# A four-block transformer kernel on one core: transposing the routing weights later, spreading a router's work over six expert steps, and the order of two multiplications

## What is computed

```
x = x + tanh(g_xattn[0]) * L0_xattn(layernorm(x), ctx)      # one attention over the context
x = x + tanh(g_ffn[0])   * L0_ffn(layernorm(x))             # ternary weights, inner width 704
x = x + tanh(g_xattn[1]) * L1_xattn(layernorm(x), ctx)      # 16 heads of 128, q and k rms-normed
x = x + tanh(g_ffn[1])   * L1_ffn(layernorm(x))             # 64 experts of width 64, 8 per token

# L1_ffn, h = its input
logits = h @ gate_w.T;  top-8;  W = softmax over the 8 chosen, 0 for the other 56
inter[e] = silu(h @ gu_w[e].gate) * (h @ gu_w[e].up) * W[:, e]
out = sum_e inter[e] @ dp_w[e].T + sigmoid(h @ sh_gate1_w.T) * shared_expert(h)
```

## Time and profile before

| | us |
|---|---|
| median of three runs | 646.48 |
| the profiled execution | 646.42 |
| its span in the trace | 644.6 |
| PE busy | 621.3 (96%) |
| DVE busy | 491.1 (76%) |
| ACT busy | 432.8 (67%) |
| POOL busy | 227.1 (35%) |
| mean DMA rate over the span | 86 GB/s |

### The profile page before, as it was taken

The page is one execution under the profiler, slowest core; times in us unless marked ns, Lnnn a source line. Parts: engine busy times, 40 slices in busy tenths (PEclk is TensorE's granted clock), DMA queues, the critical chain, the costliest instruction groups (busy, mean ns, idle before and its releaser), DMA issues.

```text
span 644.6 us, 11859 instructions
## 1 busy us (share of the span) xinstructions
PE 621.3 (96%) x3697; PEld 531.6 (82%) x3697; DVE 491.1 (76%) x1141; ACT 432.8 (67%) x1103; POOL 227.1 (35%) x262
## 2 busy tenths in 40 slices
PE   7888898999999999999989999999999999999997
PEld 5766687999999999999988887877887788888886
DVE  4999998767777778778886687877777677777775
ACT  5896998888888888888889434555444454444442
POOL 5576775766666666656654001000000000000000
PEclk9999999999999999999999999999999999999999
DMA  8420130110000000000003254436555245554440
GB/s 278 144 74 26 53 121 25 36 40 2 2 2 2 2 1 2 1 2 1 2 9 116 83 162 137 149 99 195 165 162 160 83 131 190 162 161 146 155 124 34
DMA packets 24806, 55.42 MB, mean 86 GB/s; under 512 B 4081, under 2 KB 4785, under 8 KB 24625
## 3 DMA queue, kind: packets, MB, share of 16 engines
q1 hardware_dynamic: 24752, 54.78, 27.6%
HBM read 53.45 MB, written 1.31 MB: 85 GB/s over the span
## 4 chain that ended last, share of the span: by engine, by line
PE 68%; DVE 15%; ACT 8%; issue 5%; POOL 2%; DMA 1%; SPq 0%; DVEq 0%; ACTq 0%
PE bank L285 19%; PE bank L287 19%; PE bank L286 19%; PE bank L775 3%; PE bank L750 2%; ACT front_hi L1521 2%; ACT att L1288 2%; PE bank L742 2%; DVE inter L1888 2%; DVE prod L1861 1%; DVE front_lo L2094 1%; DMA x<-in_x_tok 1%; DVE w L1650 1%; DVE stats L1603 1%; DVE amax L1707 1%
## 5 line engine op out<-in xcount | busy, mean ns | idle before, releaser
L1327 ACT ACTIVATE inter_hi<-inter 128x512 fp32r<-128x512 f32 x63 | 39.9, 634 | 142.7 <-DVE inter L1888 142.7
L285 PE MATMUL bank<-xnT_hi,front_hi 128*128 128x512 f32 (+1 forms) x260 | 102.3, 393 | 0.0
L287 PE MATMUL bank<-xnT_hi,front_lo 128*128 128x512 f32 (+1 forms) x260 | 101.7, 391 | 0.0
L286 PE MATMUL bank<-xnT_lo,front_hi 128*128 128x512 f32 (+1 forms) x260 | 101.6, 391 | 0.0
L1892 DVE TENSOR_TENSOR inter_lo<-inter,inter_hi 128x512 fp32r<-128x512 f32 x63 | 43.6, 693 | 45.8 <-ACT inter_hi L1327 45.8
L1288 ACT ACTIVATE att<-bank,shift,rq 128x256 f32<-128x256 f32 x128 | 71.3, 570 | 0.6 <-DVE shift L1781 0.6
L498 POOL TENSOR_TENSOR rk<-msq,minus_half 128x4 f32<-128x4 f32 x32 | 33.1, 1034 | 89.7 <-DVE msq L1763 89.6
L514 POOL TENSOR_TENSOR att<-att,rowinv 128x512 f32<-128x512 f32 x60 | 62.0, 1053 | 7.5 <-DVE rowinv L1791 7.5
L1774 DVE TENSOR_REDUCE rowmax<-bank 128x2 f32<-128x512 f32 x64 | 43.7, 686 | 27.0 <-PE bank L287 26.9
L1861 DVE TENSOR_TENSOR prod<-gate_s,bank 128x512 f32<-128x512 f32 x63 | 43.2, 686 | 19.7 <-PE bank L287 17.3
L287 PEld LDWEIGHTS bank<-xnT_hi,front_lo 128*128 128x128 f32 x260 | 48.8, 188 | 11.3
(11 more groups left out here) (271 smaller groups left out, 1846.8 us busy)
## 6 DMA issues: line engine op xcount, KB each, us to landing
w_all<-w_rows SPq DMA_DIRECT2D x128, 128.0 KB, 2.9
raw<-in_expert_w SPq DMA_DIRECT2D x32, 384.0 KB, 3.6
wvo_raw<-in_expert_w SPq DMA_DIRECT2D x16, 384.0 KB, 3.6
e_more<-in_expert_w SPq DMA_DIRECT2D x16, 384.0 KB, 3.6
raw<-in_head_qk SPq DMA_DIRECT2D x8, 384.0 KB, 3.7
wvo_raw<-in_head_vo SPq DMA_DIRECT2D x8, 384.0 KB, 3.1
gate_raw<-in_gate_wT SPq DMA_DIRECT2D x1, 1408.0 KB, 10.1
x<-in_x_tok SPq DMA_DIRECT2D x2, 512.0 KB, 6.2
```

The lines of the kernel that those rows point to most:

```text
L285: pe.matmul(out, l_hi, r_hi_, start=start, stop=False, skip_group_check=True)
L286: pe.matmul(out, l_hi, r_lo_, start=False, stop=False, skip_group_check=True)
L287: return pe.matmul(out, l_lo, r_hi_, start=False, stop=stop, skip_group_check=True)
L1327: act.activation(inter_hi[:, slot, :], inter[:, slot, :], ACT.Copy).then_inc(a_Ihi, 1)
```

## The change

There are three edits, of order only: no instruction is added or removed, apart from where waits stand.

1. In group 28 the first half's weights are transposed behind `values(28)`, into bank 6 (QBK) and no longer bank 7. ScalarE copies them out at the end of its group 28, behind `o_hi`, and PE waits for both copies in group 29, in front of `turn_q(31)`, which writes bank 6.
2. The second half's router has one step more: best eight in step 12, subtraction and choice in step 13, the exponentials in ScalarE's step 14, the sum in step 15, the weights in step 16, transposed and copied behind step 17.
3. In the last pair silu is multiplied by the routing weight first and by up then, and both pieces are multiplied before the first low part is made.

```diff
@@ PE, group g
+                if g == 29:
+                    pe.wait_ge(a_wk, 2)
                 if g + 2 < GROUPS:
                     pe.wait_ge(a_sqQ, 4 * min(n, GROUPS))
                     turn_q(g + 2)
...
-                if g == 28:
-                    turn_weights(0, KBK)
...
-                if g == 28:
-                    pe.wait_ge(a_wk, 2)
                 if g + 2 < GROUPS:
                     turn_k(g + 2)
...
                 values(g)
+                if g == 28:
+                    pe.wait_ge(v_Qlo, 31)
+                    turn_weights(0, QBK)
@@ PE, step q
-                if q == 16:
+                if q == 17:
                     turn_weights(1, 3)
@@ ScalarE, group g
-                if g == 28:
-                    keep_rows(0, KBK)
-                    keep_shared(0, KBK)
...
                 if n < GROUPS:
                     raw_k(n)
+                if g == 28:
+                    keep_rows(0, QBK)
+                    keep_shared(0, QBK)
@@ ScalarE, step q
-                if q == 13:
-                    silu(1, q, q)
+                if q == 14:
+                    silu(0, q, q)
                     weight_exps(1)
                     act.activation(spare[:, :], tg[:, 0:1], ACT.Silu)
                     act.wait_ge(t_D, q - 1)
-                    high_inter(1, q)
+                    high_inter(0, q)
                     split_e(q + 2)
...
-                if q == 16:
+                if q == 17:
                     keep_rows(1, 3)
                     keep_shared(1, 3)
@@ VectorE, step q
                 if q == 11:
                     take_logits(1, 0, 2)
                     take_logits(1, 1, 3)
+                if q == 12:
                     best_eight(1)
+                if q == 13:
                     shift_logits()
-                if q == 12:
                     choose()
-                if q == 14:
+                if q == 15:
                     sum_weights(1)
-                if q == 15:
+                if q == 16:
                     weights()
@@ VectorE, last pair
+            def last_loaded(half, s):
+                cols = slice(half * 256, (half + 1) * 256)
+                dve.wait_ge(a_silu, s + 1)
+                dve.wait_ge(l_wall[3], EPAIRS // 2 * 32)
+                dve.tensor_tensor(prod[:, 1, cols], gate_s[:, 1, cols], w_all[:, 3, cols], ALU.mult).then_inc(v_mul1, 1)
+
             def last_up(half, bk, s):
                 cols = slice(half * 256, (half + 1) * 256)
-                dve.wait_ge(a_silu, s + 1)
+                dve.wait_ge(v_mul1, s + 1)
                 dve.wait_ge(t_U, 2 * EPAIRS + half)
-                dve.tensor_tensor(prod[:, 1, cols], gate_s[:, 1, cols], bank[bk][:, 0:256],
-                                  ALU.mult).then_inc(v_mul1, 1)
...
+                dve.tensor_tensor(inter[:, 1, cols], prod[:, 1, cols], bank[bk][:, 0:256], ALU.mult).then_inc(v_mul2, 1)
...
-            last_up(0, UB, 2 * EPAIRS + 1)
+            last_loaded(0, 2 * EPAIRS + 1)
+            last_up(0, UB, 2 * EPAIRS + 1)
+            last_loaded(1, 2 * EPAIRS + 2)
+            last_up(1, 3, 2 * EPAIRS + 2)
             last_low(0, 2 * EPAIRS + 1)
-            last_up(1, 3, 2 * EPAIRS + 2)
-            last_loaded(1, 2 * EPAIRS + 2)
             last_low(1, 2 * EPAIRS + 2)
```

More of the change, by code:

```diff
@@ L2154, in _ @@
                     last_steps(r, r % 2, q + 2, q, q // 4)
+            def last_loaded(half, s):
[3 more added lines that the diff above has]
+                dve.tensor_tensor(prod[:, 1, cols], gate_s[:, 1, cols], w_all[:, 3, cols], ALU.mult).then_inc(v_mul1, 1)
             def last_up(half, bk, s):
                 cols = slice(half * 256, (half + 1) * 256)
-                dve.wait_ge(a_silu, s + 1)
+                dve.wait_ge(v_mul1, s + 1)
                 dve.wait_ge(t_U, 2 * EPAIRS + half)
-                dve.tensor_tensor(prod[:, 1, cols], gate_s[:, 1, cols], bank[bk][:, 0:256],
-                                  ALU.mult).then_inc(v_mul1, 1)
[L2163 to L2166, removed]
                 dve.wait_ge(a_Ihi, 2 * EPAIRS)
-                dve.tensor_tensor(inter[:, 1, cols], prod[:, 1, cols], w_all[:, 3, cols], ALU.mult).then_inc(v_mul2, 1)
+                dve.tensor_tensor(inter[:, 1, cols], prod[:, 1, cols], bank[bk][:, 0:256], ALU.mult).then_inc(v_mul2, 1)
             def last_low(half, s):
@@ L2174, in last_low @@
                                   ALU.subtract).then_inc(v_Ilo, 1)
+            last_loaded(0, 2 * EPAIRS + 1)
             last_up(0, UB, 2 * EPAIRS + 1)
-            last_loaded(0, 2 * EPAIRS + 1)
+            last_loaded(1, 2 * EPAIRS + 2)
+            last_up(1, 3, 2 * EPAIRS + 2)
             last_low(0, 2 * EPAIRS + 1)
-            last_up(1, 3, 2 * EPAIRS + 2)
-            last_loaded(1, 2 * EPAIRS + 2)
             last_low(1, 2 * EPAIRS + 2)
```

## The result

| | us |
|---|---|
| before, median of 8 runs | 646.19 (645.59 to 647.63) |
| after, median of 8 runs | 648.75 (647.38 to 650.18) |
| ratio after / before, with its 95% interval | 1.0038 [1.0028, 1.0049] |
| the profiled execution after | 647.94 |
| its span in the trace | 646.2 |

The change makes the kernel slower by 0.38%, 2.56 us between the medians. 648.6 was forecast.

The account below looks back on a forecast made before the run. PE, busy 96% of the span, was taken as the bound. Terms +0.5 + 0.07 + 2.05 + 0.1 - 0.55 = +2.17 on 646.42 gave 648.6 us; range for 8 in 10: 646.0 to 649.8.

Parts of the forecast that it names:

- PE loses the wait before `turn_k(30)` and gets it back before `turn_q(31)`: Group 28: PE gains 1.75 us by `turn_k(30)`, then gives it all back waiting for ScalarE's second copy before `turn_q(31)`.
- The rival in which the wait really goes: Group 28: ScalarE's chain is shorter than 4.62 us, PE keeps the 1.12 us, time 647.0; chance 7%.
- Pair 3 is 1.4 us late at ScalarE, 0.5 us at PE: Edit 1: pair 3's load, issued 4.6 us later, stops ScalarE about 1.4 us; +0.5 for the edit in all.
- the -0.15 for a load in time: Edit 1, rival: pair 3's load lands in time, the edit gives -0.15 us, time 647.9; chance 15%.
- The bound of +0.7: Upper bound of edit 1's cost in us, around the taken +0.5; the lower bound was -0.15.
- VectorE's chain ends at 436.30, step 18 starts at 436.84: Edit 2: the second half's weights are ready 4.33 us later, yet PE starts step 18 only 0.07 us later.
- Without a hole: Second half's router before the change: VectorE has no hole from step 12 to the weights, 18.55 us.
- `w_keep` to DRAM at 439.7, the load at 442.3, landing at 445.5, `gate(20)` at 447.4, a hole of 2.05 us: Edit 2, SyncE's queue: the later copy delays pair 20's load; PE waits 2.05 us before `gate(20)`, bounds 0 and +3.3.
- The table change and the exponentials stay hidden: Edit 2, ScalarE: both start about 420.8, end at 424.1, before step 14's product at about 424.4; bounds 0 and +0.6.
- Pairs 21 to 23 at +0.1: Edit 2: these loads are issued as much later but had more time; range 0 to 0.3 us, taken 0.1.
- Last pair -0.55: Edit 3: PE's hole of 0.54 us before the last piece goes, -0.55 us, bounds -0.7 and 0.
- Sum +2.17: All edits together: +0.5 + 0.07 + 2.05 + 0.1 - 0.55 us against the profiled execution of 646.42, giving 648.6.

## Why the prediction was right

Sign, mechanism and size came as the prediction had them, step by step:

- *PE loses the wait before `turn_k(30)` and gets it back before `turn_q(31)`*: right. 1.12 us is there, ended by `shT` again, and it comes back unchanged with both loads ahead. The rival in which the wait really goes (7%) is seen in neither profile of the change.
- *Pair 3 is 1.4 us late at ScalarE, 0.5 us at PE*: 1.55 and 0.58; the -0.15 for a load in time came out too. The term is right for that execution, but it isn't one number: the landing of that load took 3.7 to 6.1 us in these profiles, and edit 1 alone cost 1.14 at the median and 2.12 in the profile with 6.1. The bound of +0.7 was too low, since it rested on one landing. The rule that the Trainium skill gives ("DMA: Bandwidth & Descriptors", section "Anatomy of one DMA — SWDGE (gpsimd) path"; by it an estimate of 2.9 us) agrees with the 2.9 of the load issued on a quiet queue, and not with the 4.6 and 6.1 behind four spreads; the section states it for transfers issued from GpSimd, while these are issued by SyncE.
- *VectorE's chain ends at 436.30, step 18 starts at 436.84*: 436.20 and 436.73. "Without a hole" was read wrongly: each step of VectorE holds a wait of 0.76 us for `inter_hi`. The sum wasn't touched by that, since the wait is part of the 3.78 us of a step before and after.
- *`w_keep` to DRAM at 439.7, the load at 442.3, landing at 445.5, `gate(20)` at 447.4, a hole of 2.05 us*: 439.58, 442.19, 445.3, 447.24 and 1.99. PE had been at 445.25, forecast 445.36. The runs show the cause from both sides: load ahead, and the loss is gone; copy later without the longer router, and most of the loss is there.
- *The table change and the exponentials stay hidden*: the first table load starts at 420.70 (forecast 420.8) and `inter_hi` of step 14 at 424.30, after 0.28 us of waiting for VectorE, not for the tables.
- *Pairs 21 to 23 at +0.1*: PE needs 16.91 us for steps 20 to 23 where it needed 16.75 (+0.16); no hole above 0.2 us lies behind `gate(20)`.
- *Last pair -0.55*: the hole is gone, but the term was too small. PE's two pieces take 0.79 us less in the profile, and edit 3 alone gave -0.89 at the median, both beyond the bound of -0.7. The forecast took the 0.54 us of the bracket for the gain; from start to start the last piece came 0.82 us behind the last matmul of the first piece (639.24 to 640.06), and comes 0.12 us behind it now.
- *Sum +2.17*: the terms read from the profile after give 0.58 + 0.12 + 1.99 + 0.16 + 0.14 - 0.79 = +2.20 (0.12 is what PE lost up to `gate(20)` without its hole, 0.14 what lies between step 23 and the last pair, where nothing was edited). The medians gave +2.56 and, a second time, +1.65. That the first came within 0.15 us of the forecast is luck: the two rounds differ by 0.9, and the terms for pair 3 and for the last pair erred in opposite directions.

One thing the prediction lacks: what a hole of 2 us does to the clock. In edit 2 alone 7 of 10 executions had a mean clock of 0.996; the two profiled ones show about 1.5 us lost by it, and the medians were +3.76 and +3.0 with a hole of 2.05 and 1.95. In the whole change it was rarer: 4 of 16 executions had a mean clock of 0.997 or less. That fits the single edits (1.14 + 3.76 - 0.89 = 4.0) adding up to 1.4 us more than the whole. By itself each edit's hole is where it was forecast. Had the clock fallen as often in the whole change as in edit 2 alone, its median would have been 648.00 or 648.75 plus up to 1.5, so up to 649.5 or 650.25, near or above the upper end of the range (649.8). The steps were right; that this one was missing cost little by luck.

## What to carry to other kernels

Before a producer is moved later, read the in-order queue behind the wait for it: what was lost here was not the moved transpose (about 0.1 us) but the two weight loads that stood behind its copy, and a load that doesn't depend on the wait belongs in front of it. A wait for a reused bank isn't removed by taking another bank; it goes to the next writer of that one, so look for the bank whose next writer is farthest off (group 29 and bank 7 here, 1.45 us with edit 3). And take the landing time of a load in a shared queue as a spread, not as a number.

## What the chip showed beyond the forecast

- **The clock behind a hole.** After PE stood still for 1.78 or 1.89 us before `gate(20)` in edit 2 alone, the granted clock fell for some 3.4 us in both profiles, beginning 0.8 and 1.0 us after PE had restarted, with 512-column matmuls 0.43 us apart in place of 0.23. After 1.83 and 1.70 us at the same place in the two profiles of the whole change it stayed at the upper level. Of the kernel before, one execution of 81 had a mean clock as low as 0.997. With the shorter hole of the copies alone later (1.38 us) none of eleven executions had one. What tips it between otherwise like executions wasn't settled: holes of nearly the same length stand on both sides.
- **Landing times of the same load.** 384 KB took 2.9 us (pair 3, queue quiet), 2.8 to 3.2 (pair 20, behind one finished write), 3.7 to 4.9 and once 6.1 (pair 3, behind four spreads of 128 KB). Executions of edit 1 alone differ by up to 3.1 us at full clock, and those with that load ahead by 1.5; those of the kernel before beside them by 1.6 and 2.6, so the landing is not the only thing that varies.
- **Low clocks without the known hole.** Three of eleven runs with both loads ahead, two of twelve with pair 20's ahead, one of twelve of edit 1 alone and one of eleven of edit 2 with its load ahead had a mean clock of 0.997, though the profiles of these kernels show no hole before `gate(20)`. No profile caught one; their cause stays open.
